# A third pair of row buffers in the second diffusion step, with its program written out

## The reference, cut to what matters

```python
def _top_p_attention(X, W1, W2, W3):
    q = X @ W1.T @ W2.T
    k = X @ W3.T
    logits = q @ k.T / TAU
    probs = jax.nn.softmax(logits, axis=-1)
    idx = jnp.argsort(-probs, axis=-1)
    sp = jnp.take_along_axis(probs, idx, axis=-1)
    cs = jnp.cumsum(sp, axis=-1)
    keep_sorted = cs - sp < TOP_P
    rows = jnp.arange(probs.shape[0])[:, None]
    mask = jnp.zeros(probs.shape, dtype=bool).at[rows, idx].set(keep_sorted)
    A = probs * mask
    return A / jnp.maximum(A.sum(-1, keepdims=True), 1e-12)

for n in range(STEPS):            # STEPS = 2
    A = _top_p_attention(Xa, W1, W2, W3)
    Xf = R @ Xf
    Xa = A @ Xa
    Z = Z + Xf @ U1[n].T + Xa @ U2[n].T
```

## Time and profile before

| | us |
|---|---|
| median of three runs | 3150.34 |
| the profiled execution | 3151.36 |
| its span, first to last instruction | 3149.7 |
| PE busy | 2353.3 |
| DVE busy | 1947.1 |
| ACT busy | 1262.0 |
| POOL busy | 534.7 |
| second diffusion step, pairs in work | about 1590 to 2430 |

### The profile page before, as it was taken

The page is one execution under the profiler, slowest core; times in us unless marked ns, Lnnn a source line. Parts: engine busy times, 40 slices in busy tenths (PEclk is TensorE's granted clock), DMA queues, the critical chain, the costliest instruction groups (busy, mean ns, idle before and its releaser), DMA issues. The chain is left out here.

```text
span 3149.7 us, 44841 instructions
## 1 busy us (share of the span) xinstructions
PE 2353.3 (75%) x14134; PEld 1716.2 (54%) x14134; DVE 1947.1 (62%) x4750; ACT 1262.0 (40%) x2067; POOL 534.7 (17%) x1539
## 2 busy tenths in 40 slices
PE   3499999579537999969715762868637199999999
PEld 2377777468315878758404652656526044444458
DVE  5566766532437777784347678677783677777641
ACT  4455555221446666642375652657511300000000
POOL 0000000000024443430054432335410000000000
PEclk9699999889768999989767886889868599999999
DMA  1222221044100000000100000000001200000013
GB/s 43 113 93 92 92 80 62 5 166 152 40 16 12 18 26 22 20 19 19 56 0 10 10 11 9 10 13 11 15 5 46 107 1 0 0 0 0 0 43 95
DMA packets 49246, 120.76 MB, mean 38 GB/s; under 512 B 5905, under 2 KB 24625, under 8 KB 45745
## 3 DMA queue, kind: packets, MB, share of 16 engines
q1 hardware_dynamic: 49072, 118.83, 11.2%
HBM read 93.85 MB, written 24.97 MB: 38 GB/s over the span
## 5 line engine op out<-in xcount | busy, mean ns | idle before, releaser
L1818 DVE SCALAR_TENSOR_TENSOR fil_acc<-bank,fil_node,fil_acc 128x256 f32<-128x256 f32 x682 | 329.9, 484 | 110.1 <-PE bank L1886 97.5
L1291 PE MATMUL bank<-kH,qHL 128*128 128x512 f16 (+1 forms) x264 | 109.8, 416 | 373.3 <-ACT step_E L1367 354.6
L1884 PE MATMUL bank<-parts_in,fil_xTh 128*128 128x512 f16 x704 | 268.5, 381 | 0.0
L1886 PE MATMUL bank<-parts_in,fil_xTl 128*128 128x512 f16 x704 | 268.4, 381 | 0.0
L1885 PE MATMUL bank<-parts_in,fil_xTh 128*128 128x512 f16 x704 | 268.2, 381 | 0.0
L1291 PEld LDWEIGHTS bank<-kH,qHL 128*128 128x128 f16 (+1 forms) x264 | 27.1, 103 | 432.2 <-ACT step_E L1367 401.2
L1367 ACT ACTIVATE step_E<-bank 128x512 f32<-128x512 f32 (+1 forms) x264 | 131.6, 541 | 273.5 <-DVE step_recips L1745 179.8
L672 PE MATMUL bank<-V,HL 128*128 128x256 f32 x968 | 236.8, 387 | 0.2
L1483 DVE MAX8 step_top<-step_E 128x8 f32<-128x2708 f32 x44 | 131.2, 2982 | 168.7 <-ACT step_E L1367 164.8
L1388 ACT ACTIVATE step_junk<-step_E,step_first 128x2708 fp8e4<-128x2708 f32 x88 | 224.6, 2552 | 14.6 <-ACT step_first L1394 8.9
L1358 ACT ACTIVATE step_PT<-bank 128x512 f32<-128x512 f32 (+1 forms) x264 | 125.7, 578 | 244.6 <-PE bank L1281 244.6
(11 more groups left out here) (346 smaller groups left out, 4921.0 us busy)
## 6 DMA issues: line engine op xcount, KB each, us to landing
gat_A<-in_adj SPq DMA_DIRECT2D x22, 1408.0 KB, 6.1
step_a<-adjT SPq DMA_DIRECT2D x44, 352.0 KB, 3.0
gcn_raw<-in_L_W SPq DMA_DIRECT2D x16, 512.0 KB, 4.7
split<-gcn_halves SPq DMA_DIRECT2D x16, 512.0 KB, 3.4
parts_in<-split SPq DMA_DIRECT2D x4, 2048.0 KB, 19.2
adjT<-gat_a SPq DMA_DIRECT2D x22, 352.0 KB, 2.2
gcn_a<-adjT SPq DMA_DIRECT2D x22, 352.0 KB, 3.9
out_a<-adjT SPq DMA_DIRECT2D x22, 352.0 KB, 3.0
```

Of the source, the lines that this page charges most:

```text
L1291: last = pe.matmul(l_bank[n % 2][:, 0:m], cols(qHL, t, 128), k[:, c:c + m], start=part == 0, stop=part == 1)
L1818: c(dve.scalar_tensor_tensor(out=acc[k][:], in0=ps, scalar=node[k][:, n:n + 1], in1=acc[k][:], op0=ALU.mult, op1=ALU.add))
L1884: pe.matmul(w_bank[n % 4][:], xTh[k][:, x], wh[:, blk], start=c == 0, stop=False)
L1886: last = pe.matmul(w_bank[n % 4][:], xTl[k][:, x], wh[:, blk], start=False, stop=c == 1)
```

## The change

The second diffusion step gets a third pair of row buffers, laid over `core.HL` seen as f32 (2 x 2709 of 5632 elements). The buffer of pair p is then `E[p % 3][j]` in that step, chosen by `rows_of(p, q, j)`; ACT's wait before the first evacuation of pair p is for the settle of pair p - 3 instead of p - 2. As the index by threes needs p as a number, all engines' programs of that step are written out (`unrolled` in place of `pipelined`). The order of the stages, the small buffers that go by q, and the first diffusion step are as they were. All other edits hand p down to the helpers that name a row buffer.

```diff
 def diffusion_step(core, name, srcA, srcF, dstA, dstF, kH, kL, qHL, shape, adjT8, U1, U2, pending, evals, aim, bins,
-                   depth):
+                   depth, spare=None):
...
         E = [[sb(f"E{q}{j}", [128, N + 1]) for j in range(2)] for q in range(2)]
+        if spare is not None:
+            E.append([spare[:, j * (N + 1):(j + 1) * (N + 1)] for j in range(2)])
+        rows_of = lambda p, q, j: E[p % len(E) if len(E) > 2 else q][j]
+        in_order = pipelined if spare is None else unrolled
...
             if pending is None:
-                pipelined(sp, [(1, load)], T // 2)
+                in_order(sp, [(1, load)], T // 2)
...
-                pipelined(pool, [guess_0, secant_1, newton_0, guess_1, secant_0, newton_1], T // 2)
+                in_order(pool, [guess_0, secant_1, newton_0, guess_1, secant_0, newton_1], T // 2)
...
-            pipelined(pe, [*half(0, 3), *half(1, 2)], T // 2)
+            in_order(pe, [*half(0, 3), *half(1, 2)], T // 2)
...
                 if n == 0 and j == 0:
-                    reuse(act, p_ready, p)
+                    reuse(act, p_ready, p, buffers=len(E))
                 act.wait_ge(l_ready, t * NL + n + 1)
-                act.activation(E[q][j][:, c:c + m], l_bank[n % 2][:, 0:m], ACT.Copy,
+                act.activation(rows_of(p, q, j)[:, c:c + m], l_bank[n % 2][:, 0:m], ACT.Copy,
                                scale=1 / (SQ * SQ)).then_inc(l_done, 1)
...
-                dve.max(top8[:, 16 * q + 8 * j:16 * q + 8 * j + 8], E[q][j][:, 0:N]).then_inc(top8_done, 1)
+                dve.max(top8[:, 16 * q + 8 * j:16 * q + 8 * j + 8], rows_of(p, q, j)[:, 0:N]).then_inc(top8_done, 1)
...
             diffusion_step(core, "step1", A1, F1, None, None, kH, kL, qHL, shape, adjT8,
-                           L2_U1[D:, :], L2_U2[D:, :], None, 2, 15.0, 16, 48)
+                           L2_U1[D:, :], L2_U2[D:, :], None, 2, 15.0, 16, 48, core.HL[:].bitcast(F32))
```

More of the change, by code:

```diff
@@ L1223, in newton @@
                 c = begin_steps()
-                t, y = excess(c, q, j, first)
+                t, y = excess(c, p, q, j, first)
                 c(pool.tensor_scalar(pa[:, 0:1], t, goal, y, ALU.mult, ALU.subtract))
@@ L1240, in secant @@
                 c = begin_steps()
-                t, y = excess(c, q, j, second)
+                t, y = excess(c, p, q, j, second)
                 c(pool.tensor_tensor(pa[:], second[q][:, j:4:2], first[q][:, j:4:2], ALU.subtract))
@@ L1375, in exponentials @@
                 act.wait_ge(neg_max, t + 1)
-                act.activation(E[q][j][:, 0:N], E[q][j][:, 0:N], ACT.Exp, bias=at(nm, q, j),
+                act.activation(rows_of(p, q, j)[:, 0:N], rows_of(p, q, j)[:, 0:N], ACT.Exp, bias=at(nm, q, j),
                                accum_out=at(Z, q, j))
@@ L1380, in exponentials, with sums @@
                 act.activation(at(mass, q, j), at(mass, q, j), ACT.Exp, scale=-1.0).then_inc(exp_done, 1)
-            def sums(t, q, j, r, S):
+            def sums(p, q, j, r, S):
+                t = p * 2 + j
                 for i, (func, a) in enumerate(((ACT.Relu, under), (ACT.Sign, signs))):
@@ L1396, in first_sums @@
                 core.fence(act)
-                sums(t, q, j, 0, first)
+                sums(p, q, j, 0, first)
                 act.wait_ge(guessed, t * 2 + 2)
@@ L1405, in second_sums @@
                 core.fence(act)
-                sums(t, q, j, 1, second)
+                sums(p, q, j, 1, second)
             def products(p, j):
@@ L1482, in largest, with lower, candidates @@
                 core.fence(dve)
[L1483 to L1485 removed]
+                dve.max(top8[:, 16 * q + 8 * j:16 * q + 8 * j + 8], rows_of(p, q, j)[:, 0:N]).then_inc(top8_done, 1)
+            def lower(s, p, q, j):
                 S = final[q]
[L1487 to L1488 removed]
+                s(dve.scalar_tensor_tensor(out=low[:], in0=rows_of(p, q, j)[:, 0:N + 1], scalar=column(S, j),
+                                           in1=rows_of(p, q, j)[:, 0:N + 1], op0=ALU.is_lt, op1=ALU.mult,
                                            accum_out=S[:, 2 + j:3 + j]))
[L1491 removed]
+            def candidates(p, q, j):
                 s = steps(search)
[L1493 removed]
+                lower(s, p, q, j)
                 s.after()
@@ L1500, in below @@
                 dve.wait_ge(ready, p * 2 + j + 1)
-                candidates(q, j)
+                candidates(p, q, j)
             def picked(s, tiles):
@@ L1548, in threshold, with at_or_above @@
                 s.after()
-            def at_or_above(c, q, j, t, sums, op=ALU.is_ge):
-                c(dve.scalar_tensor_tensor(out=M[j][:, 0:N + 1], in0=E[q][j][:, 0:N + 1], scalar=t,
-                                           in1=E[q][j][:, 0:N + 1], op0=op, op1=ALU.mult,
+            def at_or_above(c, p, q, j, t, sums, op=ALU.is_ge):
+                c(dve.scalar_tensor_tensor(out=M[j][:, 0:N + 1], in0=rows_of(p, q, j)[:, 0:N + 1], scalar=t,
+                                           in1=rows_of(p, q, j)[:, 0:N + 1], op0=op, op1=ALU.mult,
                                            accum_out=sums[:, j:j + 1]))
@@ L1638, in split_ties @@
                 c(dve.tensor_scalar(column(quota, j), column(quota, j), 1.0, None, ALU.add))
-                c(dve.scalar_tensor_tensor(out=low[:, 0:N], in0=E[q][j][:, 0:N], scalar=column(answer[q], j),
+                c(dve.scalar_tensor_tensor(out=low[:, 0:N], in0=rows_of(p, q, j)[:, 0:N], scalar=column(answer[q], j),
                                            in1=low[:, 0:N], op0=ALU.is_equal, op1=ALU.mult))
```

60 lines of the change are left out of this document (30 added, 30 removed).

## The result

The changed kernel takes 3095.4 us (median of 4 runs, 3090.3 to 3101.4) against 3150.2 us (4 runs, 3147.4 to 3153.5): 0.9824 of the time before, 95% interval 0.9812 to 0.9837. That is 55 us less, where 57.6 were forecast. The profiled execution took 3090.3 us, the fastest of the four; its span is 3088.6.

A forecast was written before the change was run, and what follows sets the result against it. No engine's work bounds the stage; engines wait on each other in a ring. Gains of 31.6 (fast steps), 20.7 (slow) and 5.3 us (step 2), together 57.6, give 3093 us, range 3083 to 3109.

The forecast's parts named there:

- The mechanism: Second diffusion step: with three buffer pairs ACT's evacuation no longer waits for a recent settle; first MAX8's 48.8 us wait goes.
- Where the next wait would be: After the reciprocal: transposes, their copies and vT still wait for it, ahead of ACT's long passes; ACT sets second MAX8.
- step 11: Late step without logits in the trace before, used as model: transposes at +0.22 us after the reciprocal, nm at +6.50.
- The clock in the four plain steps: Steps 3, 4, 7, 9: PE's 2.2 us idle before the transposes keeps the fast clock; g 23.1 us, gain 31.6.
- rival (a): Plain steps also meet PE's slow clock: g 25.4 us there, 48.3 us gained in all, 3102 us; chance 0.20.
- g: Time from the reciprocal to the second MAX8 in steps 2 to 10: 30.42 to 31.22 us before, sum 277.5.
- the fast case: Plain steps with PE's transposes at the fast clock: nm at about +4.16 us, g 23.1 us.
- The five slow steps: Steps 2, 5, 6, 8, 10, behind repeated settles: g 25.4 us (25.9 in step 2), gains 20.7 and 5.3 us.
- The edits costed at nothing: Written-out programs of the second diffusion step and the third pair's place in memory: both taken as 0 us.
- rival (e): Third pair's memory is slow to access: 65 us more at double pass duration, 3158 us; chance 0.03.
- DVE in time for the second MAX8: DVE arrives at +21.3 or +22.9 us, before 23.1 or 25.4, so about 2 us of its wait stay.
- The new wait of finish: DVE's finish, reached at +10.98 us, waits 1.5 us for a product ready at +12.5 at PE's slow clock.

## Why the prediction was right, point by point

**The mechanism** held. The run with the wait for p - 2 puts back all of the 55 us with one number; the loop and the place of the buffers bring nothing that can be told from noise (3149.0 against 3151.2, interval to 1.0004).

**Where the next wait would be** held. The present step 11 was the right model of the new steps: transposes at +0.22 after the reciprocal, first MAX8 at +1.14 as the pass of the earlier trace rows. PE's gap before the transposes was put at 2.2 us and measured 1.9. In the steps with fast transposes `nm` was put at +4.16 and came at +4.14. That ACT sets the second MAX8 is shown by the two added instructions: 1.8 us on DVE cost nothing, 2.75 us on ACT cost more than themselves. DVE's wait there, put at about 2 us, was 2.5 to 2.7 in steps 5 to 10 and 3.4 to 5.0 in steps 2 to 4.

**The clock in the four plain steps** is the term that was mis-sized, 23.1 us against 24.3 to 25.0: 6.3 us too little in all. The prediction took 2.2 us of idle time for harmless because 1.72 us was the earlier trace rows, and because of two gaps of 3.3 us one was followed by fast matmuls. That last reading is wrong. It looked at the first matmul behind the gap, and the same timeline goes on:

```profile
1270.92 0.63 PE L1291 MATMUL bank<-kL,qHL 128*128 128x512 f16 x1
1271.35 3.13 PE L1306 MATMUL bank<-HL,step_a 128*128 128x256 f16 x14
```

The granted clock was 0.50 in 1270.9 to 1274.0 us. Both gaps of 3.3 us brought a slow stretch, one of them 0.5 us late, which is the form that steps 3 and 4 of the changed kernel then had. So the rows before showed no gap over 1.72 us that stayed fast, and more spoke for rival (a) than its chance of 0.20 says.

The forecast chose between "fast" and rival (a), "slow transposes", and the kernel did neither: in steps 7 and 9 the clock fell in the course of the transposes, in steps 3 and 4 it fell half a step later. Filling the gaps brings g to 23.33 in all four, so the gaps are the cause, and the forecast for the fast case was good: the 0.2 us over it are in the distance from `nm` to the second MAX8, 19.19 there against the 18.93 of the earlier trace rows.

**The five slow steps** erred to the other side, 25.4 and 25.9 against 24.2 to 25.3: 4.3 us. Step 11 had shown 4.95 us of transposes; here they took 4.0 to 4.7, since the clock rose before their end, at a point that differs from step to step (granted clock 0.54 in 1846.8 to 1851.6, step 5, and 0.63 in 2179.3 to 2183.4, step 10). The two errors cancel to 2.0 of 57.6 us, and 1.8 us came from behind the second MAX8, where nothing was counted. That the sum came out within 3 us was in part luck: it is better than its terms.

**The edits costed at nothing** cost nothing. Straight code: ratio 0.9989 to before, if anything faster. The third pair's memory: passes over `HL` and over the old buffers take the same time, which ends rival (e), as does the run with the wait for p - 2:

```profile
L1488 DVE MAX8 step_top<-step_E x15: 2969/2981/2983, 1593.1 to 2203.4; 128x8 f32<-128x2708 f32 x15
L1488 DVE MAX8 step_top<-HL x6: 2972/2981/2982, 1677.8 to 2087.1; 128x8 f32<-128x2708 f32 x6
```

**DVE in time for the second MAX8**, at +21.3 or +22.9 by the forecast: in step 7 it arrived at +21.79 (24.33 - 2.54). The new wait of finish in slow steps was put at 1.5 us and was 0.3 to 1.0.

## What to carry to other kernels

When a buffer is made free earlier, look for a stretch of the same trace in which the work that used it is already missing (here the last steps of the stage), and read the next wait from it: it gave the new path within 0.1 us where the clock was the same. Then ask for each new wait of the matmul engine how it stands to its clock, because a wait there can be paid twice, once as idle time and once as slow matmuls behind it, and read on past the first matmul behind a gap before calling the gap harmless. Of an engine's order, check what the moved work now stands ahead of before counting what it stands behind: 19 us were won in front of the second MAX8 and 55 lost behind it over nine steps by moving one evacuation.

## What the runs showed of the hardware

In the changed kernel, from the settle of pair 0 to that of pair 9, PE was busy 405 of 601 us. Each plain step there had gaps of 1.65, 1.9 and 1.5 to 2.0 us and one stretch of 3 to 4 us at the lower of PE's two clock levels, 1.2 GHz. The stretch began up to 0.8 us after a gap of 1.9 or 2.0 us, in step 4 behind three matmuls at the fast level. With all gaps filled down to about 0.7 us or less, none of twelve plain steps had such a stretch; with only the gap before the reciprocal filled, steps 3 and 4 kept theirs and steps 7 and 9 lost it.

The length of one gap doesn't decide alone: in the changed kernel the transposes behind 1.95 us (step 3) were fast and those behind 1.89 us (step 7) slow. Why steps 3 and 4 fell later than 7 and 9 is open: the second trace of the same program moved one of the four. Which of the gaps are needed is open too.

The Trainium skill (TensorE: Matmul & The Clock Gate, section on why this matters for your kernels) warns of gaps longer than these. Here gaps shorter than its bound cost 1.0 to 1.7 us a plain step (g of 24.33 and 25.00 against 23.33 with the gaps filled).

An added ACT pass of 2.75 us cost 4.3 us in each of 11 steps on average (47 / 11): it made a gap of PE longer, and slow matmuls followed.
